# Deeper rings around the edge loop of a graph attention layer: three buffers for the aggregation's operands, eight for the transposed edge features

## The reference

```python
h = relu(layernorm(x))
xm = h @ W_n2m.T                       # 6250 x 128
xl, xr = xm @ Wl.T + bl, xm @ Wr.T + br
e = (rbf @ W_r2m.T) @ We.T             # per edge, 128
u = leaky_relu(xl[src] + xr[dst] + e, 0.2)
logits = einsum('ehd,hd->eh', u, att)  # per edge and head
p = exp(logits - segment_max(logits, dst)[dst])
alpha = p / segment_sum(p, dst)[dst]
out = segment_sum(xl[src] * alpha, dst) + bias
return x + out @ W_m2n.T
```

## Time and profile before

| | |
|---|---|
| three runs | 3231.31, 3236.71, 3242.29 us |
| median | 3236.71 us |
| the profiled execution's own time | 3200.59 us |
| its span | 3198.8 us |
| mean granted TensorE clock in it | 0.828 |
| busy: TensorE, GpSimd, ScalarE, VectorE | 2501.8, 1631.7, 1552.9, 1470.5 us |

### The profile page before, as it was taken

The page is one execution under the profiler, slowest core; times in us unless marked ns, Lnnn a source line. Parts: engine busy times, 40 slices in busy tenths (PEclk is TensorE's granted clock), DMA queues, the critical chain, the costliest instruction groups (busy, mean ns, idle before and its releaser), DMA issues. The chain is left out here.

```text
span 3198.8 us, 62156 instructions
## 1 busy us (share of the span) xinstructions
PE 2501.8 (78%) x11639; PEld 1541.6 (48%) x11640; DVE 1470.5 (46%) x4279; ACT 1552.9 (49%) x4428; POOL 1631.7 (51%) x1819
## 2 busy tenths in 40 slices
PE   5613878888788888888887888878888878887987
PEld 3401545545455555445454555445554545444565
DVE  6401444444444444445444444444444444444577
ACT  3301545555455445445545455554545544544672
POOL 4874455555455455555555455555555555555203
PEclk9755988888888888878888788888888887888999
DMA  4221333333333333333333333333333333333317
GB/s 144 83 56 48 85 79 82 85 81 83 81 81 79 84 85 82 82 82 87 82 79 88 85 81 79 85 79 77 85 83 91 86 78 85 82 82 78 78 30 132
DMA packets 317109, 263.45 MB, mean 82 GB/s; under 512 B 173619, under 2 KB 289637, under 8 KB 316438
## 3 DMA queue, kind: packets, MB, share of 16 engines
q1 hardware_dynamic: 254222, 142.33, 17.1%
q0 software_dynamic: 57632, 113.02, 14.7%
q10 hardware_dynamic: 4840, 3.68, 0.4%
HBM read 247.39 MB, written 16.89 MB: 83 GB/s over the span
## 5 line engine op out<-in xcount | busy, mean ns | idle before, releaser
L811 POOL DMA_INDIRECT xl_g<-xl_table,src_tab x1612 | 1532.5, 951 | 1353.8 <-DVE msg L1010 871.7
L881 PE MATMUL banks<-msg,onehot 128*128 128x177 f32 x3416 | 771.9, 375 | 58.0 <-issue 51.7
L881 PEld LDWEIGHTS banks<-msg,onehot 128*128 128x128 f32 x3416 | 633.7, 226 | 265.7 <-issue 235.4
L1027 DVE SCALAR_TENSOR_TENSOR uT<-banks,uT 128x512 f32<-128x512 f32 x427 | 294.4, 689 | 922.1 <-ACT uT L943 480.5
L836 PE MATMUL banks<-attrT,Wc 32*128 32x512 f32 x854 | 548.2, 724 | 145.0 <-DMA attrT<-in_attr_cols 117.2
L927 ACT ACTIVATE distance<-iota_n,minus_slot 128x128 f32<-128x128 f32 x1708 | 550.4, 388 | 119.4 <-issue 119.1
L1005 DVE TENSOR_TENSOR msg<-xl_g,banks 128x256 f32<-128x256 f32 x854 | 320.8, 417 | 571.5 <-remote 409.6
L832 PE MATMUL banks<-onehotT,xr_parts 128*128 128x256 bf16 x2562 | 419.6, 303 | 196.1 <-issue 168.4
L943 ACT ACTIVATE uT<-banks 128x512 f32<-128x512 f32 x427 | 249.7, 585 | 648.4 <-remote 445.3
L905 ACT ACTIVATE xl_z<-xl_g 128x256 f32 x854 | 310.9, 407 | 224.2 <-issue 162.0
L932 ACT ACTIVATE onehot<-distance 128x512 f32<-128x512 f32 x427 | 269.0, 630 | 299.1 <-remote 164.1
(11 more groups left out here) (199 smaller groups left out, 1430.3 us busy)
## 6 DMA issues: line engine op xcount, KB each, us to landing
slot_bc<-slot_dram SPq DMA_DIRECT2D x427, 128.0 KB
attrT<-in_attr_cols SPq DMA_DIRECT2D x854, 32.0 KB
rbf<-in_attr_rows SPq DMA_DIRECT2D x854, 32.0 KB
xl_g<-xl_table,src_tab POOLq DMA_INDIRECT x1612
masks<-masks_dram SPq DMA_DIRECT2D x108, 96.5 KB
out<-in_x SPq DMA_DIRECT2D x16, 336.0 KB
out<-result POOLq DMA_DIRECT2D x6, 896.0 KB, 8.4
xl_table<-lr_sb SPq DMA_DIRECT2D x49, 64.0 KB, 1.5
```

Of the source, the lines that this page charges most:

```text
L811: pool.indirect_dma_start(out=xl_g[:, g % PRING, i], out_offset=None, in_=xl_table, in_offset=bass.IndirectOffsetOnAxis(ap=src_tab[:, j:j ...
L881: mm = nc.tensor.matmul(U_ps[j % 2][:, h], onehot[:, j % 2, t], msg[:, j % 2, t], start=i == 0, stop=i == PT - 1)
L1027: nc.vector.scalar_tensor_tensor(out=uT[:, s % URING], in0=z_ps[s % 2], scalar=SLOPE, in1=uT[:, s % URING], op0=ALU.mult, op1=ALU.add).the ...
```

## The change

`onehot` and `msg` get three buffers each (SUM_RING), and the two waits ahead of their writers ask for one aggregation less. `attrT` gets eight buffers instead of three: it is now one tile of 128 rows with two columns of buffers, and the 32 rows of step s lie at partitions 32 x (s mod 4). L836 takes the copy of the weights in the same rows of `Wc`, and names its row group by `tile_position`. The waits at L784 and L835 follow TRING.

```diff
--- before.py
+++ after.py
@@ -35,13 +35,15 @@
 SLOPE = 0.2
 RING = 24
 SRING = 4
-TRING = 3
+TRING = 8
+TROWS = P // D_RBF
 ARING = 4
 PRING = 64
 ZRING = 3
 FREED = 2
 FREE_ROW = 4
 MRING = 2
+SUM_RING = 3
 UNROLL = 48
 BATCH = 8
 BATCHES = -(-STEPS // BATCH)
@@ -680,14 +682,14 @@
         rbf = sb("rbf", [P, ARING, TILES * D_RBF])
         slot_bc = sb("slot_bc", [P, SRING, GROUP], BF16)
         masks = sb("masks", [P, MRING, MASKS], BF16)
-        attrT = sb("attrT", [D_RBF, TRING, GROUP])
+        attrT = sb("attrT", [P, TRING // TROWS, GROUP])
         xl_g = sb("xl_g", [P, PRING, PT, D_MSG])
         xl_z = sb("xl_z", [P, ZRING, SPLIT, PT, D_MSG])
         onehotT = sb("onehotT", [P, 4, GROUP], BF16)
         uT = sb("uT", [P, URING, GROUP])
         distance = sb("distance", [P, TILES, P])
-        onehot = sb("onehot", [P, 2, TILES, P])
-        msg = sb("msg", [P, 2, TILES, AGG])
+        onehot = sb("onehot", [P, SUM_RING, TILES, P])
+        msg = sb("msg", [P, SUM_RING, TILES, AGG])
         run_ends = sb("run_ends", [P, 4])
         run_max = sb("run_max", [P, PIECE])
         low = sb("low", [P, PIECE])
@@ -782,8 +784,9 @@
                 if inside(k, STEPS):
                     if inside(k - TRING, STEPS):
                         sp.wait_ge(z_done, k - TRING + 1)
+                    to = slice(s % TROWS * D_RBF, (s % TROWS + 1) * D_RBF)
                     for h in range(SPLIT):
-                        sp.dma_start(attrT[:, s % TRING, h * PIECE:(h + 1) * PIECE],
+                        sp.dma_start(attrT[to, s % TRING // TROWS, h * PIECE:(h + 1) * PIECE],
                                      attr_cols[one(now[h])].rearrange("a k e -> (a k) e")
                                      ).then_inc(turned_in[s % TRING], 16)
                 if inside(k - LATE, STEPS):
@@ -833,7 +836,9 @@
                                              onehotT[:, n4, h * PIECE:(h + 1) * PIECE],
                                              start=h == 0 and part == 0, stop=False)
                     pe.wait_ge(turned_in[s % TRING], (r * (UNROLL // TRING) + s // TRING + 1) * FULL)
-                    nc.tensor.matmul(z, Wc[0:D_RBF], attrT[:, s % TRING], start=False, stop=False)
+                    of = slice(s % TROWS * D_RBF, (s % TROWS + 1) * D_RBF)
+                    nc.tensor.matmul(z, Wc[of], attrT[of, s % TRING // TROWS], start=False, stop=False,
+                                     tile_position=(s % TROWS * D_RBF, 0))
                     pe.wait_ge(xl_ready, SPLIT * (k + 1))
                     for h in range(SPLIT):
                         for i in range(PT):
@@ -878,7 +883,7 @@
                     for h in range(SPLIT):
                         for i in range(PT):
                             t = h * PT + i
-                            mm = nc.tensor.matmul(U_ps[j % 2][:, h], onehot[:, j % 2, t], msg[:, j % 2, t],
+                            mm = nc.tensor.matmul(U_ps[j % 2][:, h], onehot[:, j % SUM_RING, t], msg[:, j % SUM_RING, t],
                                                   start=i == 0, stop=i == PT - 1)
                     mm.then_inc(agg_done, 1)
                 b = batch_at(s, r, TURN)
@@ -927,13 +932,13 @@
                         nc.scalar.activation(distance[:, t], iota_n[:], ACT.Abs,
                                              bias=minus_slot[:, one(TILES * (k - LAG + 1) + t)]).then_inc(dist_ready, 1)
                     act.wait_ge(dist_ready, TILES * (k - LAG + 2))
-                    if inside(k - LAG - 1, STEPS):
-                        act.wait_ge(agg_done, k - LAG)
-                    nc.scalar.activation(onehot[:, m % 2], distance[:], ACT.Relu, scale=-1.0, bias=1.0
+                    if inside(k - LAG + 1 - SUM_RING, STEPS):
+                        act.wait_ge(agg_done, k - LAG + 2 - SUM_RING)
+                    nc.scalar.activation(onehot[:, m % SUM_RING], distance[:], ACT.Relu, scale=-1.0, bias=1.0
                                          ).then_inc(oh_ready, TICK)
                 if inside(k - LAG + 1, STEPS):
                     act.wait_ge(loads[m % ARING], (r * (UNROLL // ARING) + (s - LAG + 1) // ARING + 1) * FULL)
-                    nc.scalar.activation(msg[:, m % 2, :, CNT:AGG],
+                    nc.scalar.activation(msg[:, m % SUM_RING, :, CNT:AGG],
                                          rbf[:, m % ARING].rearrange("p (t k) -> p t k", t=TILES), ACT.Copy
                                          ).then_inc(attr_ready, TICK)
                 if inside(k, STEPS):
@@ -997,9 +1002,9 @@
                     if m % BATCH == 0:
                         b = r * (UNROLL // BATCH) + (s - LAG + 1) // BATCH
                         dve.wait_ge(wT_done, b + 1)
-                    if inside(k - LAG - 1, STEPS):
-                        dve.wait_ge(agg_done, k - LAG)
-                    to = msg[:, m % 2, :, 0:MSG].rearrange("p t (h c) -> p t h c", c=HC)
+                    if inside(k - LAG + 1 - SUM_RING, STEPS):
+                        dve.wait_ge(agg_done, k - LAG + 2 - SUM_RING)
+                    to = msg[:, m % SUM_RING, :, 0:MSG].rearrange("p t (h c) -> p t h c", c=HC)
                     for h in range(SPLIT):
                         two = slice(h * PT, (h + 1) * PT)
                         nc.vector.tensor_tensor(to[:, two, :, 0:D_HEAD],
```

## The result

The change makes the kernel slower: 3385.98 us in the median of four runs (3379.00 to 3406.68), against 3234.01 us before (four runs beside them, 3206.04 to 3242.29). The ratio is 1.0491, 95% interval 1.0450 to 1.0531. The profiled execution took 3379.0 us with a span of 3377.2 and a granted clock of 0.802.

What follows compares the result with a forecast made beforehand. The prediction took TensorE, busy 78% of the span, to bound the kernel. Ring of eight 20 us, three buffers 10 and row groups 0 made 30 us off 3236.7: 3207 us, range 3155 to 3258.

Steps and rivals of the forecast that it cites:

- What bounds the kernel: Loop: TensorE sets the pace, idle 18% of the long stretch; SyncE's attrT transfers are late by its queue's own pace.
- Ring of eight, 20 us: SyncE's wait at L786: eight attrT buffers remove 59.9 us of blocked queue in the stretch; 20 us won, ends 0 and 71.
- the gates behind L786: SyncE's waits at the slot_bc and rbf issues stay, so its queue gets about one step further ahead, not five.
- the 80 to 100 I named: Sign at L836: TensorE's wait for attrT falls from 117.2 us to 80 to 100 in the stretch, not to zero.
- the lead pays in full: Rival for SyncE's queue and VectorE's waits: all 71 and 32 us return, TensorE's clock adds 10; 3124 us, chance 0.05.
- Three buffers, 10 us: Waits before onehot and msg: up to 0.80 us saved at some TensorE waits for VectorE; 10 us won, ends 0 and 32.
- Rival 3, GpSimd's stream starts sooner: GpSimd's gathers: earlier msg frees their ring, so they run beside and slow ScalarE's work; 3276 us, chance 0.12.
- 46 steps x 1.5 us = 69 us: Price of the earlier gathers: ScalarE's distance operations 1.5 us slower in each of 46 loop steps, 69 us at most.
- the sign named for this rival: ScalarE's idle time for issue before L905 and L927 grows if the earlier gather stream costs; no size given.
- As many gathers as before, so slow time moved here is missing elsewhere: Argument against the earlier gather stream costing: the number of gathers is unchanged, so slow time only moves; no size given.
- Row groups, 0: L836 on row groups by turns: no gain or loss, term 0; ends 105 us saved in the stretch, 131 us lost.
- TensorE's waits for VectorE: TensorE's waits for end_row and msg, 91.7 us in 34 waits in the stretch, get shorter by some us in all.

Runs made afterwards that it cites:

- e2: The changed kernel with two buffers instead of three for onehot and msg, attrT's ring of eight kept; 3239.61 us, 0.9969 of the kernel before.
- e3: The changed kernel with two onehot and msg buffers and SyncE's old wait for z of step k-3, leaving the row groups; 3245.64 us, 0.9999 of before.
- e1: The kernel before with three buffers for onehot and msg and both new waits, attrT unchanged; 3404.07 us, 1.0511 of before.
- f4: The changed kernel itself, run again on the third chip against the kernel before; 3393.74 us, 1.0507 of before.
- f3: The kernel before with three onehot and msg buffers, both new waits, and GpSimd released behind the sums instead of msg; 3233.31 us, 0.9999 of before.
- f2: The kernel before with three onehot and msg buffers, only VectorE's msg wait one aggregation earlier, on the third chip; 3403.48 us, 1.0541 of before.
- e6: The kernel before with three onehot and msg buffers, only VectorE's msg wait one aggregation earlier, on the second chip; 2291.41 us against 2293.85 before.
- e4: The kernel before with three onehot and msg buffers but both old waits, on the second chip; 2291.82 us against 2293.85 before.

## Why the prediction was wrong

- *What bounds the kernel.* That TensorE sets the pace and idles 18% of the stretch was right as arithmetic, and so was the reading of SyncE: its transfers are late because it is slow while GpSimd streams. The step that failed began there. Having seen a queue slowed by the stream, I took it for a trait of that queue. The traces show it on SyncE, TensorE, VectorE and ScalarE, and it was to be seen before: ScalarE's `distance` in the earlier trace rows, and 315.4 us `remote` before L943.
- *Ring of eight, 20 us.* Measured by `e2` against `e3`: 0.9969 and 0.9999, so 0.3% or 10 us, and each interval takes in nothing at all. The sign may be right; the size is half of what I took, though 20 us is not excluded. That the gates behind L786 would hold SyncE was right in the changed kernel only, and half by name (38 us each at `slot_bc` and `masks`, nothing at `rbf`); in `e2` it hardly waits at all, and TensorE waits 152.7 us for `attrT`, not the 80 to 100 I named. In the changed kernel these waits vanished, which was to be the sign that the lead pays in full; it is no such sign, since `e1` loses them too.
- *Three buffers, 10 us.* The failed term: its ends were 0 and 32 us won, and it measured 156 us lost (`e1`). The working held for what it looked at: the wait before `msg` is gone, and stands before the sums and the leaky relu. It took the wait for idle time to be filled, and followed only what VectorE and ScalarE do behind it. But VectorE's wait also held GpSimd, by way of `msg` and the ring of 64 pieces. While it stood, the stream ran dry, the count came through, `msg` was written at once, and the next gathers followed 1.84 us after the wait in the mean. With three buffers `msg` is already written when the count is late. VectorE then stands ahead of the sums instead, and the next gathers have to wait for the `msg` of the turn after: 5.11 us.
- *Rival 3, GpSimd's stream starts sooner.* The right place and the right direction, given 0.12. Its price was wrong in kind: 46 steps x 1.5 us = 69 us for ScalarE's slower `distance`, taken from one stretch. ScalarE's idle time before `distance` hardly moved, 116.7 us in 369 steps before and 125.3 in 346 after, so the sign named for this rival did not show either. What costs are counts that come late on both sides of TensorE, and the pauses of GpSimd behind them, 0.45 us a step over all 427. "As many gathers as before, so slow time moved here is missing elsewhere" was the argument against it. It supposes that the gathers alone set the price; the streams do take the same time, and the pauses between them do not. The 46 steps are themselves a guess: they divide 227.1 us by the one wait of 5.76 us in the earlier trace rows, where the profile counts 74 waits.
- *Row groups, 0.* Right: 0.9999 (`e3`), the L840 matmul took 727 ns in the mean where L836 took 722, its weight load 208 ns where it was 205. The Trainium skill (TensorEngine Tiling (Array Packing), Key Properties) says that a change of tiling mode drains TensorE; no drain shows here, since `e3` and the kernel before come out equal. Whether L836 had been in that mode already, no run tells.
- *TensorE's waits for VectorE* were to get shorter by some us, and no such thing shows. For `end_row` and `msg` (L861 and L896) they are 75.7 + 29.0 = 104.7 us after, where they were 91.7; in `f4`, the same kernel again, 38.5 + 38.8 = 77.3.

How the stream delays the counts is not settled. That it does is in the order of time, and that the release of the gathers is the cause of the loss is shown by `f3`. The link between the two, that the release now comes a turn after VectorE's wait instead of right behind it, rests on the traces and not on a run that moved its place in the turn alone.

## What to carry to other kernels

A wait that looks like lost time may be what keeps another engine back. Before taking one away, follow every count that the waiting engine gives after it, and ask what starts earlier. If that is a stream of indirect transfers, keep its release right behind the wait and move the work alone: `f3` lost nothing where `e1` lost 5%, though it gained nothing either. And a kernel tuned on one chip can have its gain or loss only there: an earlier `msg` cost 5.4% on one kind (`f2`) and nothing on the other (`e6`, the same code). The changed kernel itself was not run on a chip of the faster kind.

## What the runs showed of the hardware

- The same kernel takes some 3240 us on two chips (3247.92, 3237.62) and 2294 us on two others (2293.85, 2293.05). GpSimd is busy for nearly the same time on either kind (1631.7 us in the kernel before, 1636.3 in `e4`). The slower kind has TensorE at a mean clock of 0.80 to 0.83, the faster at 0.96. Beside that the kinds differ in what a stream of gathers does to the other engines; whether the clock is a cause of the longer time or comes of it, no run tells.
- On the slower kind, counting all records of the kernel before, waits and register operations too, between 400 and 2900 us: SyncE starts 2.1 instructions a microsecond while GpSimd streams and 4.2 otherwise, VectorE 2.8 and 4.3, ScalarE 3.6 and 5.1. On the faster kind, under an unbroken stream, it is 4.0, 4.8 and 5.8. Part of the difference may be the engines' waits for one another.
- It grows within a stream. In the 29 streams of twelve gathers of the kernel after, SyncE, VectorE, ScalarE and TensorE's matmuls together start 20 instructions a microsecond beside the first gather, 12 beside the fifth, 4 beside the eighth and 2 beside the twelfth. In the third 1.25 us behind that they start 21 again.
- TensorE is hit too, with no wait in the program: a bf16 matmul of 256 columns every 2.80 us in the middle of a group, where six take 0.82 us otherwise, and one instruction of either kind every 1.40 us.
